# Two attention layers and 32 routed experts on one core: routing one turn earlier, and the last three sequences in an order of their own

## The chip, the cores and the metric

The kernel runs on one core of a Trainium2 chip. The metric is the time of one execution on the device in microseconds (us), lower is better. The engines of the core are named as in the profile: PE is TensorE (PEld its weight loads), DVE is VectorE, ACT is ScalarE, POOL is GpSimd and SP is SyncE, which here only issues DMAs. They run side by side, each through a list of instructions of its own, and wait for each other by semaphores that count up.

## The reference

A decoder layer on 16 sequences of 256 tokens with 256 values each, in float32:

```python
def reference(x, ctx_1024, ...):               # x, ctx: (16, 256, 256) float32
    # attention 1, one head
    q, k, v = x @ Wq.T + bq, x @ Wk.T + bk, x @ Wv.T + bv
    qk = einsum('bsd,btd->bst', q, k)
    theta = 0.5 + 0.2 * sigmoid(qk) + 0.15 * tanh(qk) + 0.1 * relu(qk)
    x1 = layernorm(x + (softmax(theta) @ v) @ Wo.T + bo)
    # attention 2 against ctx, 16 heads of 16, in chunks of 64 positions
    ...
    x2 = layernorm(x1 + out @ out_proj_w.T + out_proj_b)
    # feed-forward: 32 experts in 4 groups, 4 chosen per token, and a shared one
    scores = sigmoid(x2 @ router_weight.T)
    # best 2 groups by the sum of their top 2 scores, then the best 4 experts in them
    topk_w = scores[chosen] / sum(scores[chosen]) * 2.5
    mixed = sum_k topk_w[k] * (silu(x2 @ gate_w[k].T) * (x2 @ up_w[k].T)) @ down_w[k].T
    shared = (silu(x2 @ sg.T) * (x2 @ su.T)) @ sd.T
    return layernorm(x2 + mixed + shared)
```

## The kernel before

**Two halves.** The first half takes the 16 sequences through both attentions, the shared expert's first product and the routing; each token's row is written four times, once per chosen expert, into a list in memory (`routed`). Then tables are made that say which rows belong to which block (`vec_tables`, `pe_tables`). The second half runs 140 blocks of rows through the experts (`pe_gu`, `pe_down`), scatters the results to `y` and adds up and normalizes them (`vec_out`). The change is in the first half and in the tables; from the first expert block on the code is the same.

**Turns and lags.** The first half is a loop of turns `t` from 0 to 21. In each turn an engine does certain steps of several sequences, each with its own lag: sequence `t` gets its first attention (steps `z`, `vo`, `scores1`, `tanh`, `pr`, `prT`, `av1`, `x1`, and `k`, `v` from ctx), sequence `t-1` gets `norm1`, `x1T` and `q`, sequence `t-2` its second attention (`scores2`, `mxa`, `sha`, `mxb`, `shb`, `pTa`, `pTb`, `den`, `av2`, `rden`, `spread`, `o`, `out2`, `x2`). `x2` is DVE's sum and statistics before the second layernorm. Sequence `t-3` gets `rs2` on POOL (the inverse root) and `norm2` on ACT, late in the turn. Sequence `t-4` is routed: `x2T` (transposes on PE, L339, then a copy on ACT), `router` (L538), `sc`, `route`, `choice`, `rank` (L563), `key`, and `gate` (L547) with `hs1`; sequence `t-5` gets `up` (L556) and `hs2`, and the eight scatters of a sequence (`scattera`, `scatterb`, POOL) follow at lags of 5 and 6. A step named with a number, `key(15)`, is that step of that sequence. Turns 0 to 15 start new sequences; turns 16 to 21 only drain, here called the tail. `live(i)` leaves out what lies outside 0 to 15.

**What sets the order.** Each engine has its own list, written out by hand in the loop bodies (PE L733 to L783, ACT L956 to L996, DVE L1292 to L1337, POOL L1394 to L1406). Within an engine nothing overtakes (PE may only load weights early). So a step starts when the one ahead of it on its engine is through and its semaphores have arrived. PSUM banks are shared between steps: `vo` and `gate`, `av2` and `out2` use bank 6, `x2T`, `router` and `up` bank 7, `z`, `scores1`, `prT` and `rank` bank 5, `scores2` banks 0 to 3. For that reason there are waits such as `after(e, SEM["v_ve2"], i - 2)` in `pe_vo`: bank 6 must have been read by `x2` of sequence `t-3`.

**The end of the half.** `vec_tables` starts when `pe_tables` has counted the rows; that matmul waits for `key(15)` and `hs2(15)`. The blocks' loads on SP wait for the tables and for all scatters to have landed.

## Time and profile before

| | us |
|---|---|
| median of 3 runs | 793.93 |
| lowest, highest | 793.92, 798.06 |
| the profiled execution | 795.5 |
| its span | 793.6 |
| TensorE busy | 742.6 (94%) |
| VectorE busy | 564.5 (71%) |
| ScalarE busy | 476.0 (60%) |
| GpSimd busy | 349.8 (44%) |

Times inside the profile are counted from the start of its span; 1.9 us of the execution lie around the span. In the span the turns 0 to 15 end at 409.66 (where `scores2(14)` starts), the tail ends with `key(15)`, and the first expert block's matmuls start at 493.04.
### The profile page before, as it was taken

What the parts mean: (1) busy time and instruction counts of PE and PEld (TensorE: products, weight loads), DVE (VectorE), ACT (ScalarE), POOL (GpSimd) and SP (SyncE); (2) the same over time, 40 slices, a digit from 0 to 9 for tenths busy, and PEclk for the clock granted to TensorE, in tenths of its full rate; (3) what the DMA queues carried; (4) which work ended last, traced back from release to release, by engine and by line L of the source; (5) the groups of instructions that cost most, each with busy time, mean ns of one, the idle gap of its engine ahead of it and who ended that gap; (6) DMA issues with size and microseconds to landing.
All of it is one profiled execution on the core that took longest, in us unless ns stands there. A gap on an engine that the chain in (4) does not pass through costs nothing.

```text
span 793.6 us, 21763 instructions
## 1 busy us (share of the span) xinstructions
PE 742.6 (94%) x8276; PEld 627.1 (79%) x8276; DVE 564.5 (71%) x2038; ACT 476.0 (60%) x1110; POOL 349.8 (44%) x418
## 2 busy tenths in 40 slices
...
GB/s 257 158 100 58 65 98 88 133 122 115 136 136 120 132 117 126 123 124 133 82 51 106 141 103 120 248 273 262 280 301 277 274 271 266 246 222 102 391 402 236
DMA packets 75884, 138.84 MB, mean 175 GB/s; under 512 B 10882, under 2 KB 42114, under 8 KB 75651
## 3 DMA queue, kind: packets, MB, share of 16 engines
...
q10 hardware_dynamic: 4368, 4.20, 1.5%
...
## 4 chain that ended last, share of the span: by engine, by line
PE 82%; DVE 7%; DMA 5%; issue 2%; SPq 2%; ACT 2%; POOL 1%; ACTq 0%; DVEq 0%
PE banks L604 13%; PE banks L339 11%; PE banks L624 7%; PE banks L412 4%; PE banks L444 4%; PE banks L547 3%; PE banks L389 3%; PE banks L435 3%; PE banks L380 3%; PE banks L425 3%; PE banks L556 3%; PE banks L521 3%; PE banks L397 3%; DMA w_expert_tile<-y 2%; PE banks L513 2%; PE banks L487 2%
## 5 line engine op out<-in xcount | busy, mean ns | idle before, releaser
L1409 POOL DMA_INDIRECT y<-yb_tile,idcol_tile x140 | 134.2, 959 | 106.5 <-DVE yb_tile L1257 99.1
L604 PE MATMUL banks<-xbT_tile,wgu_tile 128*128 128x128 f32 x1024 | 136.6, 277 | 0.0
L604 PEld LDWEIGHTS banks<-xbT_tile,wgu_tile 128*128 128x128 f32 x1024 | 125.7, 193 | 0.4 <-ACT xbT_tile L809 0.3
L1257 DVE SCALAR_TENSOR_TENSOR yb_tile<-banks,rowsb_tile 128x256 f32<-128x256 f32 x140 | 67.7, 484 | 80.6 <-PE banks L624 52.7
L948 ACT ACTIVATE wgu_tile<-w_expert_tile 128x512 f32 x128 | 79.8, 623 | 24.2 <-DVE tab_i_tile L1232 17.3
L1387 POOL DMA_INDIRECT routed<-row_tile,idx_tile x64 | 62.5, 977 | 67.3 <-PE banks L457 51.8
L624 PE MATMUL banks<-w_expert_tile,hb_tile 128*128 x256 | 78.4, 388 | 0.7 <-DVE hb_tile L1244 0.6
L936 ACT ACTIVATE gb_tile<-banks 128x128 f32<-128x128 f32 x140 | 38.8, 277 | 63.5 <-PE banks L604 57.0
L1381 POOL DMA_INDIRECT routed<-row_tile,idx_tile x64 | 61.6, 963 | 33.8 <-issue 18.5
L1362 POOL TENSOR_TENSOR rs_tile<-ve_tile,half_neg_tile 128x2 f32<-128x2 f32 x16 | 11.1, 693 | 143.5 <-DVE ve_tile L1051 143.5
L809 ACT ACTIVATE xbT_tile<-banks 128x256 f32<-128x256 f32 x140 | 52.9, 378 | 9.3 <-PE banks L339 7.3
L339 PE MATMUL banks<-const_tile,rowsb_tile 128*128 128x128 f32 x280 | 55.0, 279 | 2.1 <-DMA rowsb_tile<-routed 2.1
L339 PEld LDWEIGHTS banks<-const_tile,rowsb_tile 128*128 128x128 f32 x280 | 38.3, 142 | 20.8 <-issue 6.2
L722 ACT ACTIVATE w_expert_tile<-w_expert_tile,fnmr_tile,frs_tile 128x256 f32<-128x256 f32 x32 | 17.6, 593 | 49.1 <-DVE fnmr_tile L702 49.1
L624 PEld LDWEIGHTS banks<-w_expert_tile,hb_tile 128*128 128x128 f32 x256 | 38.7, 191 | 6.8 <-issue 6.6
L1244 DVE TENSOR_TENSOR hb_tile<-hb_tile,banks 128x128 f32<-128x128 f32 x140 | 40.1, 287 | 4.8
L1241 DVE SCALAR_TENSOR_TENSOR hb_tile<-gb_tile,banks 128x128 f32<-128x128 f32 x140 | 39.3, 281 | 3.8 <-ACT gb_tile L936 3.8
L1357 POOL TENSOR_TENSOR xc_tile<-x_sb_tile,c_out_tile 128x256 f32<-128x256 f32 x32 | 22.6, 733 | 42.7 <-ACT x_tile L901 22.5
L715 POOL TENSOR_TENSOR frs_tile<-fve_tile,fhalf_tile 128x2 f32<-128x2 f32 (+1 forms) x17 | 17.9, 1055 | 43.2 <-DVE fve_tile L697 43.2
L556 PE MATMUL banks<-x2T_tile,w_early_tile 128*128 128x256 f32 x128 | 35.1, 423 | 1.3 <-ACT sc_tile L921 1.3
L679 PE MATMUL banks<-w_expert_tile,const_tile 128*128 128x512 f32 (+1 forms) x68 | 30.6, 577 | 4.2 <-DMA w_expert_tile<-y 4.1
L444 PE MATMUL banks<-w_expert_tile,w_early_tile 128*128 128x256 f32 x128 | 32.0, 391 | 0.2 <-issue 0.2
...
## 6 DMA issues: line engine op xcount, KB each, us to landing
...
rowsb_tile<-routed SPq DMA_DIRECT2D x128, 129.0 KB
...
```

Of the source, the lines that this page charges most:

```text
L339: return e.transpose(o, i, ident)
L444: m = e.matmul(bank[0][:, db * S:(db + 1) * S], w_cross[:, k, 0, db * P:(db + 1) * P], x1T[:, k, :], start=k == 0, stop=k == DK - 1)
L556: m = e.matmul(bank[7][:, b * S:(b + 1) * S], w_shared_in[:, k, 2 * P + b * P:3 * P + b * P], x2T[i % 2][:, k, :], start=k == 0, stop=k == ...
L604: m = e.matmul(o[:, h * P:(h + 1) * P], wgu[s % WG][:, k * D + h * EI:k * D + (h + 1) * EI], xbT[s % 2][:, k * P:(k + 1) * P], start=k == ...
L624: m = e.matmul(o[:, 0:D], hb[s % 4][:, :], w_flat[:, bass.ds(w.pop(g) + 2 * D, D)], start=True, stop=True)
L809: e.activation(o, i, ACT.Copy).then_inc(SEM[done], 1)
L948: e.activation(wgu[s % WG][:, :], w_flat[:, bass.ds(w.pop(n), DK * D)], ACT.Copy)
L1244: e.tensor_tensor(hb[s % 4][:, :], hb1[s % 2][:, :], bank[2 + s % 4][:, EI:2 * EI], ALU.mult)\
L1257: e.scalar_tensor_tensor(yb[s % YS][:, :], bank[6 + s % 2][:, 0:D], rowsb[s % ROWS][:, D:D + 1], rowsb[s % ROWS][:, 0:D], ALU.mult, ALU.ad ...
L1381: e.indirect_dma_start(routed, bass.IndirectOffsetOnAxis(ap=idx[i % 2][:, 0, k:k + 1], axis=0), row[i % 2][:, k, 0, :], None).then_inc(SEM ...
L1387: e.indirect_dma_start(routed, bass.IndirectOffsetOnAxis(ap=idx[i % 2][:, 1, k:k + 1], axis=0), row[i % 2][:, k, 1, :], None).then_inc(SEM ...
L1409: e.indirect_dma_start(y, bass.IndirectOffsetOnAxis(ap=idcol[n % ROWS][:, :], axis=0), yb[n % YS][:, :], None).then_inc(SEM[f"st_y{n % YS} ...
```

## The change

**Lag three.** In turns 0 to 15 all that follows the second attention moves up. `norm2(t-3)` becomes ACT's first step of the turn, `x2T`, `router`, `gate`, `up`, `rank` and the steps on DVE take sequence `t-3` instead of `t-4` (`up` and `hs2` instead of `t-5`), the scatters take `t-4` and `t-5`. POOL does `rs2(t-3)` first. On ACT `norm1(t-1)` moves from ahead of `sha` to behind `shb`. `pe_x1T` gets a wait for `a_x1`, `pe_av2` waits for the latest `hs1`, `pe_gate` and `pe_up` lose waits that their new places make needless.

**The tail written out.** The loop ends at turn 15. What is left of the last three sequences, A = 13, B = 14 and C = 15, stands behind it as a list for each engine. `x1T(15)` and `q(15)` go to banks 4 and 5. The tables' first matmul becomes `pe_counts`, which sums `macc` and `msel` itself, so it no longer waits for `key(15)` and `hs2(15)`; the tables use banks 2 and 3. `hs1(15)` and `hs2(15)` go into `vec_tables` on DVE, `up(15)` stands on PE between `pe_counts` and the tables' second matmul. The semaphore of the stores of `hs` is split in two, and SP's list is cut in the same way. The core of the diff:

```diff
         def pe_x1T(e, i):
+            e.wait_ge(SEM["a_x1"], i + 1)
+            if i == C:
+                e.wait_ge(SEM["a_v"], nseq)
+            o = bank[4 if i == C else 0]
...
         def pe_av2(e, i):
-            after(e, SEM["v_h1"], i - 1)
+            after(e, SEM["v_h1"], i)
...
         def pe_gate(e, i):
-            after(e, SEM["a_vo"], min(i + 5, nseq))
-            after(e, SEM["v_ve2"], min(i + 2, nseq))
+            after(e, SEM["a_vo"], min(i + 4, nseq))
...
         def pe_up(e, i):
-            after(e, SEM["a_sc"], min(i + 2, nseq))
-            after(e, SEM["v_hs"], i)
+            e.wait_ge(SEM["a_sc"], i + 1)
...
+        def pe_counts(e):
+            e.matmul(bank[3][0:E, 0:1], macc[:, T - 1, :], c("ones")[:, 0:1], start=True, stop=False)
+            e.matmul(bank[3][0:E, 0:1], msel[:, T - 1, :], c("ones")[:, 0:1], start=False, stop=True)\
+                .then_inc(SEM["p_tab"], 1)
+
         def pe_tables(e):
 
-            e.wait_ge(SEM["v_key"], nseq)
-            e.wait_ge(SEM["v_hs"], nseq)
-            e.matmul(bank[7][0:E, 0:1], macc[:, 0, :], c("ones")[:, 0:1], start=True, stop=True)\
-                .then_inc(SEM["p_tab"], 1)
             e.wait_ge(SEM["v_place"], 1)
...
-            for t in range(nseq + 6):
+            for t in range(nseq):
                 if live(t - 2):
                     pe_scores2(e, t - 2)
-                if live(t - 4):
-                    pe_x2T(e, t - 4)
                 if live(t):
                     pe_z(e, t)
-                if live(t - 4):
-                    pe_router(e, t - 4)
...
+            pe_scores2(e, B)
+            pe_x1T(e, C)
+            pe_x2T(e, A)
+            pe_q(e, C)
+            pe_router(e, A)
+            pe_gate(e, A)
+            pe_pTa(e, B)
+            pe_up(e, A)
...
+            pe_out2(e, B)
+            pe_scores2(e, C)
+            pe_x2T(e, B)
+            pe_router(e, B)
+            pe_gate(e, B)
+            pe_pTa(e, C)
+            pe_pTb(e, C)
+            pe_up(e, B)
+            pe_den(e, C)
...
+            pe_out2(e, C)
+            pe_rank(e, B)
+            pe_x2T(e, C)
+            pe_router(e, C)
+            pe_gate(e, C)
+            pe_rank(e, C)
+            pe_counts(e)
+            pe_up(e, C)
             pe_tables(e)
...
+            act_norm1(e, C)
+            act_norm2(e, A)
+            act_x1T(e, C)
+            act_sha(e, B)
...
+            act_norm2(e, B)
+            act_sha(e, C)
+            act_x2T(e, B)
...
+            vec_hs1(e, C, ch)
             e.wait_ge(SEM["p_tab"], 2)
...
+            vec_hs2(e, C, ch)
             e.wait_ge(SEM["p_tab"], 4)
...
+            vec_route(e, B, ch)
+            vec_rden(e, C, ch)
+            vec_hs1(e, B, ch)
+            vec_route2(e, B, ch)
+            vec_o(e, C, ch)
+            vec_choice(e, B, ch)
+            vec_hs2(e, B, ch)
+            vec_x2(e, C, ch)
+            vec_key(e, B, ch)
+            vec_route(e, C, ch)
+            vec_route2(e, C, ch)
+            vec_choice(e, C, ch)
+            vec_key(e, C, ch)
             vec_tables(e, ch)
...
+            for t in range(nseq):
                 if live(t - 3):
                     pool_rs2(e, t - 3)
+                if live(t - 5):
+                    pool_scatterb(e, t - 5)
+                if live(t - 4):
+                    pool_scattera(e, t - 4)
```

Left out are the rest of the lists, the bank numbers in the tables, and the split semaphore.

**ScalarE, from the last steps of one steady turn into the next.** L915 (after: L958) is `norm2`, L873 (L915) `q`, L832 (L874) `v`, L809 on x2T (L851) its copy, L814 (L856) `z`, L921 `sc`, L901 `norm1`, L879 (L922) `sha`. Before:

```order
L915 ACTIVATE x20_tile<-xc20_tile,nmr20_tile,rs20_tile 128x256 x2
L873 ACTIVATE qT_tile<-banks,b_cross_tile 128x256 x2
L832 ACTIVATE vM1_tile<-banks 64x8x16 x8
L809 ACTIVATE x2T0_tile<-banks 128x512
L814 ACTIVATE zT_tile<-banks,g_bias_tile 128x256 x2
L921 ACTIVATE sc_tile<-banks 128x64
L901 ACTIVATE x11_tile<-xc_tile,nmr1_tile,rs1_tile 128x256 x2
L879 ACTIVATE sha_tile<-sha_tile 128x1024
```

After:

```order
L915 ACTIVATE qT_tile<-banks,b_cross_tile 128x256 x2
L874 ACTIVATE vM1_tile<-banks 64x8x16 x8
L958 ACTIVATE x21_tile<-xc21_tile,nmr21_tile,rs21_tile 128x256 x2
L856 ACTIVATE zT_tile<-banks,g_bias_tile 128x256 x2
L922 ACTIVATE sha_tile<-sha_tile 128x1024
L851 ACTIVATE x2T1_tile<-banks 128x512
L883 ACTIVATE vo_tile<-banks 128x256 x2
```

`norm2` went from ahead of `q` and `v` of the turn before to the place between `v` and `z`, and `norm1` and `sc` left the stretch ahead of `sha`.

**TensorE, the start of turn 14.** L457 (after: L466) is `scores2`, L339 (L341) on x2 is `x2T`, L380 (L382) `z`, L538 (L547) `router`, L389 (L391) `vo`, L397 (L399) `scores1`, L556 (L563) `up`, L555 is `gate`. Before:

```order
L457 MATMUL banks<-kM0_tile,qT_tile 64x128 x32
L339 MATMUL banks<-const_tile,x20_tile 128x128 x4
L380 MATMUL banks<-xT_tile,g_qk_tile 128x256 x4
L538 MATMUL banks<-w_router_tile,x2T0_tile 128x32 x4
L389 MATMUL banks<-g_vo_tile,xT_tile 128x257 x4
L397 MATMUL banks<-xT_tile,zT_tile 128x256 x4
L556 MATMUL banks<-x2T1_tile,w_early_tile 128x256 x4
```

After:

```order
L466 MATMUL banks<-kM0_tile,qT_tile 64x128 x32
L382 MATMUL banks<-xT_tile,g_qk_tile 128x256 x4
L391 MATMUL banks<-g_vo_tile,xT_tile 128x257 x4
L341 MATMUL banks<-const_tile,x21_tile 128x128 x4
L399 MATMUL banks<-xT_tile,zT_tile 128x256 x4
L547 MATMUL banks<-w_router_tile,x2T1_tile 128x32 x4
L341 MATMUL banks<-const_tile,sha_tile 128x128 x8
L555 MATMUL banks<-x2T1_tile,w_early_tile 128x256 x4
L563 MATMUL banks<-x2T1_tile,w_early_tile 128x256 x4
```

`x2T` went behind `vo`, `router` behind `scores1`, and `up` behind `gate`, which are now of the same sequence.

**TensorE, the tail, from `scores2(15)` on.** Names as above; L339 (L341) on sha and shb are `pTa(15)` and `pTb(15)`. Before:

```order
L457 MATMUL banks<-w_expert_tile,qT_tile 64x128 x32
L339 MATMUL banks<-const_tile,x21_tile 128x128 x4
L538 MATMUL banks<-w_router_tile,x2T1_tile 128x32 x4
L556 MATMUL banks<-x2T0_tile,w_early_tile 128x256 x4
L339 MATMUL banks<-const_tile,sha_tile 128x128 x8
L547 MATMUL banks<-x2T1_tile,w_early_tile 128x256 x4
L339 MATMUL banks<-const_tile,shb_tile 128x128 x8
```

After:

```order
L466 MATMUL banks<-w_expert_tile,qT_tile 64x128 x32
L341 MATMUL banks<-const_tile,x20_tile 128x128 x4
L547 MATMUL banks<-w_router_tile,x2T0_tile 128x32 x4
L555 MATMUL banks<-x2T0_tile,w_early_tile 128x256 x4
L341 MATMUL banks<-const_tile,sha_tile 128x128 x8
L341 MATMUL banks<-const_tile,shb_tile 128x128 x8
L563 MATMUL banks<-x2T0_tile,w_early_tile 128x256 x4
```

Ahead of `pTa(15)` there now stand `x2T`, `router` and `gate` of sequence 14, where before there were `x2T` and `router` of 13 and `up` of 12, and `up(14)` stands between `pTb(15)` and the `den` that follows.

## Rows read from the trace of the kernel before

**Rows 1.** Busy time by stretch: turns 3, 4 and 15 (first: the columns).
```profile
core 0: us, PE busy (x) PEld busy (x) DVE busy (x) ACT busy (x) POOL busy (x), PEclk, DMA share, GB/s
65.04:89.72 24.68, 21.72 (x353) 18.57 (x352) 13.42 (x31) 15.89 (x38) 4.51 (x8) 1.00 0.24 82
...
89.72:117.14 27.42, 25.14 (x378) 21.85 (x377) 20.42 (x76) 19.59 (x44) 4.51 (x8) 1.00 0.23 74
...
383.28:409.66 26.38, 26.38 (x386) 23.33 (x385) 23.24 (x81) 18.52 (x40) 12.32 (x16) 1.00 0.17 59
```

**Rows 2.** Timeline, TensorE, turn 13: start, duration, engine, line, tile, count [idle before].
```profile
329.64 1.21 PE L457 MATMUL banks<-w_expert_tile,qT_tile 32*64 32x128 f32 x64
330.77 0.66 PE L339 MATMUL banks<-const_tile,x_tile 128*128 128x128 f32 x4
331.27 1.89 PE L380 MATMUL banks<-xT_tile,g_qk_tile 128*128 128x256 f32 x8
333.00 0.97 PE L538 MATMUL banks<-w_router_tile,x2T_tile 128*128 128x32 f32 x8
333.81 1.98 PE L389 MATMUL banks<-g_vo_tile,xT_tile 128*128 128x257 f32 x8
335.63 1.89 PE L397 MATMUL banks<-xT_tile,zT_tile 128*128 128x256 f32 x8
337.35 1.89 PE L556 MATMUL banks<-x2T_tile,w_early_tile 128*128 128x256 f32 x8
```

**Rows 3.** Timeline, TensorE, turn 3: the spread, with the idle time inside it.
```profile
85.73 0.42 PE L513 MATMUL banks<-rden_tile,const_tile 128*32 128x64 f32 x12 [1.65 <-issue]
```

**Rows 4.** Timeline, VectorE, start of turn 13: last step of x2's statistics.
```profile
332.29 0.17 DVE L1051 TENSOR_SCALAR ve_tile<-ag_tile 128x2 f32<-128x2 f32 x1
```

**Rows 5.** Timeline, GpSimd, turn 12: rs2 and nmr2.
```profile
316.80 0.76 POOL L1368 TENSOR_TENSOR rs_tile<-ve_tile,half_neg_tile 128x2 f32<-128x2 f32 x1
317.64 0.20 POOL L1370 TENSOR_TENSOR nmr_tile<-neg_tile,rs_tile 128x2 f32<-128x2 f32 x1
```

**Rows 6.** Timeline, ScalarE: norm2 in turn 11, z in turn 13.
```profile
299.71 1.10 ACT L915 ACTIVATE x_tile<-xc_tile,nmr_tile,rs_tile 128x256 f32<-128x256 f32 x2
...
333.20 0.84 ACT L814 ACTIVATE zT_tile<-banks,g_bias_tile 128x256 f32<-128x256 f32 x2 [1.13 <-PE banks L380]
```

**Rows 7.** Timeline, ScalarE, turn 16: copy of the first transposed shares, exp of the second.
```profile
418.49 1.02 ACT L887 ACTIVATE sha_tile<-banks 128x1024 f32<-128x1024 f32 x1 [2.55 <-PE banks L339]
419.42 1.05 ACT L883 ACTIVATE shb_tile<-shb_tile 128x1024 f32<-128x1024 f32 x1
```

**Rows 8.** Busy time by stretch: turn 16, turn 17, the drain in two pieces.
```profile
409.66:430.09 20.43, 16.27 (x326) 13.58 (x325) 16.87 (x63) 11.94 (x21) 10.03 (x12) 1.00 0.20 71
430.09:449.07 18.98, 14.46 (x314) 11.99 (x314) 16.64 (x62) 8.73 (x11) 13.95 (x16) 1.00 0.38 129
449.07:461.28 12.21, 7.99 (x34) 6.38 (x32) 9.47 (x51) 4.20 (x6) 8.68 (x10) 0.79 0.48 159
461.28:479.94 18.66, 13.56 (x42) 10.39 (x43) 11.87 (x62) 3.22 (x4) 8.96 (x11) 0.59 0.26 93
```

**Rows 9.** Timeline, TensorE: first transposes of turn 17; rank of sequence 14.
```profile
437.83 1.06 PE L339 MATMUL banks<-const_tile,sha_tile 128*128 128x128 f32 x8 [1.88 <-DVE shb_tile L1082]
...
460.37 0.69 PE L563 MATMUL banks<-msel_tile,const_tile 128*128 128x64 f32 x2 [3.22 <-DVE wraw_tile L1150]
```

**Rows 10.** Timeline, VectorE: routing of sequence 14; last instruction of key(15).
```profile
452.08 0.19 DVE L1106 TENSOR_SCALAR sc_tile<-sc_tile 128x64 f32<-128x64 f32 x1
...
456.07 0.18 DVE L1135 MATCH_REPLACE8 er_tile<-ev_tile,tmp_tile 128x36 f32<-128x36 f32 x1
...
458.42 0.33 DVE L1141 TENSOR_SCALAR msel_tile<-er_tile 128x64 f32<-128x64 f32 x1
...
477.72 0.42 DVE L1188 TENSOR_REDUCE row_tile<-mine_tile 128x8 f32<-128x256 f32 x1
```

**Rows 11.** Timeline, GpSimd: the last scatter of sequence 15.
```profile
487.25 0.96 POOL L1387 DMA_INDIRECT routed<-row_tile,idx_tile  x1 [0.30 <-issue]
```

**Rows 12.** Timeline, TensorE: the first expert block.
```profile
493.04 1.26 PE L339 MATMUL banks<-const_tile,rowsb_tile 128*128 128x128 f32 x4 [2.12 <-DMA rowsb_tile<-routed]
```

More of the change, by code:

```diff
@@ L863, in act_x1T @@
             e.wait_ge(SEM["p_x1T"], i + 1)
-            copy(e, x1T[:, :, :].rearrange("p a b -> p (a b)"), bank[0][:, :], "a_x1T")
+            copy(e, x1T[:, :, :].rearrange("p a b -> p (a b)"), bank[4 if i == C else 0][:, :], "a_x1T")
         def act_x2T(e, i):
@@ L996, in _ @@
                     act_v(e, t)
+            act_norm1(e, C)
+            act_norm2(e, A)
+            act_x1T(e, C)
+            act_sha(e, B)
+            act_x2T(e, A)
+            act_q(e, C)
+            act_sc(e, A)
+            act_pTa(e, B)
+            act_shb(e, B)
+            act_gates(e, A)
+            act_pTb(e, B)
+            act_row(e, A)
+            act_num(e, B)
+            act_norm2(e, B)
+            act_sha(e, C)
+            act_x2T(e, B)
+            act_sc(e, B)
+            act_pTa(e, C)
+            act_shb(e, C)
+            act_gates(e, B)
+            act_pTb(e, C)
+            act_num(e, C)
+            act_row(e, B)
+            act_norm2(e, C)
+            act_x2T(e, C)
+            act_sc(e, C)
+            act_gates(e, C)
+            act_row(e, C)
             e.wait_ge(SEM["v_tab"], 1)
@@ L1204, in vec_tables @@
             e.tensor_scalar(rows_full[:, :], place[:, E:E + 1], float(P), None, ALU.mult)
+            vec_hs1(e, C, ch)
             e.wait_ge(SEM["p_tab"], 2)
-            ch(e.tensor_scalar(above[:, :], bank[7][0:E, 8:8 + E], order[:, 0:1], None, ALU.is_gt))
+            ch(e.tensor_scalar(above[:, :], bank[3][0:E, 8:8 + E], order[:, 0:1], None, ALU.is_gt))
             ch(e.tensor_reduce(rank[:, :], above[:, :], AX.X, ALU.add))
-            ch(e.tensor_tensor(rank[:, :], bank[7][0:E, 8 + E:9 + E], rank[:, :], ALU.add))
+            ch(e.tensor_tensor(rank[:, :], bank[3][0:E, 8 + E:9 + E], rank[:, :], ALU.add))
             ch(e.scalar_tensor_tensor(nblk[:, 1:2], rank[:, :], float(FULL), over[:, :], ALU.is_ge, ALU.mult))
@@ L1290, in _ @@
             e.tensor_copy(c_bqbk[:, :], bank[2][:, 0:1]).then_inc(SEM["v_setup"], 1)
-            for t in range(nseq + 6):
+            for t in range(nseq):
                 if live(t - 2):
@@ L1465, in _ @@
             e.dma_start(w_shared_out[:, :, :], d["w_shared_out"]).then_inc(SEM["ld_w"], 16)
-            for t in range(nseq + 6):
+            for t in range(nseq):
                 if live(t) and t > 0:
@@ L1474, in _ @@
                     load_c(e, t)
-                if live(t - 6):
-                    store_hs(e, t - 6)
+                if live(t - 4):
+                    store_hs(e, t - 4)
                 if 0 < t <= nseq - LATE:
                     load_rest(e, t - 1)
-                if nseq < t <= nseq + LATE:
-                    load_rest(e, t - 1 - LATE)
+            store_zero(e, B)
+            store_zero(e, C)
+            store_hs(e, A - 1)
+            store_hs(e, A)
+            for i in range(nseq - LATE, nseq):
+                load_rest(e, i)
+            store_hs(e, B)
+            store_hs(e, C)
             e.wait_ge(SEM["v_adr"], 1)
```

165 lines of the change are left out of this document (109 added, 56 removed).

## The prediction

> **What bounds the kernel now.** I read the busy times by stretch first. In a steady turn TensorE has no idle time at all: turn 15 is 26.38 us long and 26.38 us busy, at the full clock, while VectorE has 3.1 us to spare, ScalarE 7.9 and GpSimd 14.1 [rows 1]. Two kinds of stretch are different. Turns 3 and 4 have 2.96 and 2.28 us of TensorE idle time, because routing has not begun or `up` is missing [rows 1]. And the tail, from 409.66 to the end of `key(15)` at 477.72 + 0.42 = 478.14 [rows 8, 10], takes 68.5 us for some 50 us of TensorE time, part of it at the half clock: PEclk is 0.79 and 0.59 in the drain [rows 8]. Behind `key(15)` come its eight scatters, the last issued at 487.25 [rows 11], then the first block's matmuls at 493.04 [rows 12], 14.9 us after `key(15)`. From there on nothing changes. So the change is worth what it does to two lengths: turns 2 to 15, and the tail up to `key(15)`.
>
> **Part 1: work goes from the tail into the turns.** Turn 3 gets a whole routing: `x2T` 0.50, `router` 0.81, `gate` and `up` 1.73 each (the starts of the rows that follow each other [rows 2]), `rank` about 0.4, so 5.2 us; turn 4 gets one `up`, 1.7. Turn 3 will be as long as a full turn, 26.4, plus what idle time stays. Of its 2.96 us, 1.65 is a pause inside the spread that has no releaser [rows 3]; I keep it. The other 1.3 is filled. That makes 28.0 for 24.68, **+3.3**. Turn 4: 26.4 plus a like pause of 1.65 makes 28.0 for 27.42, **+0.6**. A turn that is bound by TensorE hides nothing of this. It would be free only if the tail gets shorter by as much.
>
> **Part 2: the chain at the start of each turn.** This is the term I weigh most. At lag four `norm2` had most of a turn of slack. At lag three it must run at once. Counted from the start of `scores2`, 329.64 [rows 2]: the statistics of x2 end at 332.29 + 0.17 = 332.46, so +2.8 [rows 4]. That does not move, as it hangs on `rank` and `key` at the end of the turn before. Then GpSimd's two steps, 316.80 to 317.84, 1.04 [rows 5]: +3.9. ScalarE stands in front of `norm2` from then on, 1.10 [rows 6]: +5.0. Behind `norm2` in its queue is `z`, 0.84 [rows 6], which before began at 333.20 = +3.6 and now begins at about +4.9, as adjacent ScalarE instructions overlap by 0.1: done at +5.7. TensorE meanwhile has `scores2` 1.13, `z` 1.73, `vo` 1.82, through at +4.7 [rows 2]. It waits for `norm2` until +5.0 (0.3), does `x2T` until +5.5, and waits for `z` until +5.8 (0.25) before `scores1`. So about 0.6 us of TensorE idle time in each of turns 3 to 15: 13 x 0.6 = **+7.8**. Behind `scores1` I find no further wait: `router` has its copy of x2T at about +7.2 and starts at +7.5; `norm1` is done by about +12.5 and `x1T` starts at +14.4. The bounds: 0 if GpSimd and ScalarE come 0.6 us earlier than these rows say; 1.2 a turn (+15.6) if `vo`, whose wait for the same statistics at +2.8 falls within 0.1 us of its turn at +2.9, is late as well and each hand-over costs 0.1 more.
>
> In turn 2 nothing is routed and TensorE is early, so that `norm1` behind the copy and the exp of the shares, 1.02 and 1.05 [rows 7], makes `x1T` late: between 0 and 2.1, I take **+1.0**. The sum of the turns: 3.3 + 0.6 + 7.8 + 1.0 = **+12.7**.
>
> **Part 3: the tail.** I lay it out in three legs against before [rows 8].
>
> Leg 1, `scores2(14)` to `scores2(15)`: 20.43 before. Now `x1T(15)` goes early but its copy stands behind `norm2(13)` on ScalarE (+5.0, then 0.6), and from +5.0 the engines alternate: 5.7 us of TensorE work (`x2T`, `q`, `router`, `gate`, `pTa`), copy and exp of the shares (2.1, [rows 7]), transposes, copy, `den`, `rden`, `choice`, `o`, `out2` end at about +21.1. **+0.7**.
>
> Leg 2, `scores2(15)` to the end of `x2(15)`: before 430.09 to 452.1, 22.0 [rows 8, 10]. Then `pTa(15)` started 7.7 after `scores2(15)`, when VectorE's shares were there [rows 9]. Now ahead of it stand `x2T(14)`, which must wait for statistics, GpSimd and `norm2(14)` (+6.4 in the leg), the copy behind `sha(15)` (+8.2), `router` and `gate`, so `pTa(15)` starts at about +10.7; and `up(14)`, 1.73, stands between `pTb(15)` and `den`, where ScalarE's copy (1.0) would hide but part. The leg takes about 25.8: **+3.8**.
>
> Leg 3, end of `x2(15)` to the end of `key(15)`: 452.1 to 478.14, 26.0. In it sequence 14 is routed first and 15 after. Now 15 goes directly: GpSimd 1.04 and `norm2` 1.10 [rows 5, 6]; `x2T` to the start of routing as 449.07 to 452.08, 3.0; routing 452.08 to 456.25, 4.2; `choice` to `rank` 458.42 to 460.37, 1.95 [rows 8 to 10]; `rank` and `key` to the end about 3.7 by the same steps before, at the half clock. Sum 15.0, and 0.9 for a `router` at the half clock: 15.9. **-10.1**.
>
> So the legs give 0.7 + 3.8 - 10.1 = -5.6, with legs 1 and 2 at the full clock. I do not believe in that clock. Before, the clock went down in the drain and the engine met a 3.22 us gap that ended at half speed [rows 8, 9]. By my layout the new tail has gaps of about 3 us behind `x1T(15)`, 5.3 behind `scores2(15)`, 3.3 ahead of `x2T(15)`. Each of the first two should cost some 2 us (about 4 us of work at half speed until the clock is back), and the work between `pTb(15)` and `out2(15)`, 6.6 us, may fall low as well: between 0 and 6.6, I take 1.5. **+5.5**, bounds 0 and 10.6. The tail is then -0.1, about as long as before. The Trainium skill's page "TensorE: Matmul & The Clock Gate", Part 1, says that the throttled state is the default and that activity releases it; the trace agrees so far that PEclk is 1.00 only where the engine is kept busy. By that rule the gaps cost what I add here; if it did not hold the tail would be the 5.6 us shorter.
>
> **Part 4: the tables.** `counts` no longer waits for `hs2(15)`, and `hs1(15)`, `hs2(15)` fill waits. That would bring the tables some 1.9 us forward from `key(15)`. I cost it at nothing, because the eight scatters of sequence 15 cannot start before `key(15)`: the last is issued 9.1 us after it [rows 10, 11] and must land before SP loads. The 14.9 us stay. If the tables were the later of the two, up to 1.9 would be won.
>
> **The sum.** 12.7 in the turns and -0.1 in the tail, +12.6. The profiled execution's 795.5 becomes 808.1. It lay 1.6 above the median of 793.93, so the median should come to **806.5**.
>
> **The rivals.**
> *A, no stall at the turn's start* (0.10): the chain of part 2 fits into its slack. For it: 0.6 us is a small difference of rows that are each 0.1 wide. Against: three engines in series without any reserve. 806.5 - 7.8 = 798.7.
> *B, the clock stays up in the tail* (0.08): legs 1 and 2 lose nothing, leg 3 some 2 less. 806.5 - 7.5 = 799.0. For it: in turn 17, with 14.46 of 18.98 us busy, PEclk was 1.00 [rows 8]. Against: gaps of 5 us were not in that turn.
> *C, faster: the written-out tail is bound by TensorE's work and not by hand-overs* (0.08). Its place is legs 1 and 2: if the new order covers every hand-over, they take no more than TensorE was busy in turns 16 and 17, 16.27 and 14.46 us [rows 8], in place of 46.9, and the clock stays up. The tail is 30.7 + 15.9 = 46.6, which is 21.9 shorter: 793.9 + 12.7 - 21.9 = 784.7. It decides from a tail under 55.8 us, where it outweighs the turns. For it: 18 us of the old tail were idle on TensorE. Against: each sequence's second attention goes through seven hand-overs, and only two sequences are left to alternate.
> *D, a worse stall*, 1.2 us a turn (0.08): 814.3.
> *E, the shift does nothing*: turns stay at 26.4 and the tail gains what turns 3 and 4 lose. It lands within 4 us of 793.93 (0.06).
>
> **How the numbers follow.** The forecast, 806.5, with its own bounds of 801 to 813, has 0.60. 0.5% is 4 us, about what a measurement of this kernel can tell from no change. Faster than 790: C and a little from E and the unseen, 0.10. Within: E, parts of A and B, 0.12. Slower than 798: the forecast, D and the larger part of A and B, 0.78. A range from 796 to 815 leaves out C, E and the far ends.
>
> **What would show it.** In the profile after: the start of `scores2(14)` at about 422 instead of 409.66; turns of 27.0; on TensorE a wait of 0.2 to 0.4 for `z` ahead of `scores1` and another for `norm2` in each turn; from there to the end of `key(15)` about 68 us, with PEclk below 1 already in the first half of it; 14.9 us from `key(15)` to the first block. Turns of 26.4 would make part 2 wrong; a tail of under 60 us would make part 3 wrong; a first block nearer than 13.5 us to `key(15)`, part 4.

## The result and the profile after

| | before | after |
|---|---|---|
| median | 795.22 us (4 runs beside after, 793.92 to 798.06) | 809.44 us (4 runs, 805.82 to 811.79) |
| ratio | | 1.0166, 95% interval 1.0139 to 1.0192 |
| span of the profiled execution | 793.6 us | 807.9 us |
| start of `scores2(14)`, end of the turns | 409.66 | 422.34 |
| from there to the end of `key(15)`, the tail | 68.48 us | 70.47 us |
| end of `key(15)` to the first expert block | 14.90 us | 14.88 us |

The change makes the kernel slower by 1.7%. In the two profiled executions 12.7 us of it lie in the turns, 2.0 in the tail, and nothing behind it. First the turns. Busy time by stretch, kernel after, turns 2, 3, 4 and 15 (columns as in [rows 1]); turns 3, 4 and 15 answer to the rows of before there:

```profile
43.34:66.90 23.56, 21.89 (x352) 18.63 (x353) 11.14 (x24) 15.62 (x39) 4.46 (x8) 1.00 0.28 86
66.90:93.96 27.06, 26.63 (x385) 23.40 (x385) 21.56 (x77) 19.22 (x44) 4.56 (x8) 1.00 0.23 64
93.96:121.85 27.89, 27.23 (x385) 23.32 (x385) 22.31 (x81) 18.84 (x42) 8.65 (x12) 1.00 0.31 101
...
395.24:422.34 27.10, 26.93 (x386) 23.19 (x385) 23.08 (x81) 18.79 (x42) 12.80 (x16) 1.00 0.17 61
```

Turn 15 is 27.10 us long instead of 26.38, with the same 385 or 386 matmuls. Its 0.17 us of idle time does not show this; the starts do. Timeline of TensorE, start of turn 15 (columns as in [rows 2]), and of ScalarE:

```profile
395.24 1.21 PE L466 MATMUL banks<-w_expert_tile,qT_tile 32*64 32x128 f32 x64
396.38 1.99 PE L382 MATMUL banks<-xT_tile,g_qk_tile 128*128 128x256 f32 x8
398.21 1.98 PE L391 MATMUL banks<-g_vo_tile,xT_tile 128*128 128x257 f32 x8
400.28 0.66 PE L341 MATMUL banks<-const_tile,x_tile 128*128 128x128 f32 x4
401.00 1.99 PE L399 MATMUL banks<-xT_tile,zT_tile 128*128 128x256 f32 x8
```
```profile
399.14 1.09 ACT L958 ACTIVATE x_tile<-xc_tile,nmr_tile,rs_tile 128x256 f32<-128x256 f32 x2 [3.35 <-POOL nmr_tile L1476]
400.14 0.82 ACT L856 ACTIVATE zT_tile<-banks,g_bias_tile 128x256 f32<-128x256 f32 x2
```

`vo` holds TensorE for 1.82 us [rows 2], so it is free at 400.03; `x2T` starts at 400.28, 5.04 into the turn, when `norm2` is done. `x2T` holds it for 0.50, until 400.78; `scores1` starts at 401.00, when `z` is done. Of the two waits, 0.25 and 0.22 us, the profile's idle column shows only 0.17, because the ends of matmuls are modelled. One has to subtract starts. Done for every step of turn 15 in both kernels, this gives the whole difference: `vo` and `x2T` with the waits behind them 0.25 and 0.23, `z` 0.10 (1.83 where it follows `scores2`, 1.73 where it followed `x2T`), `scores1` 0.11, `pTa` 0.03, together 0.72.

The tail, busy time by stretch: leg 1 (turn 16's place), leg 2 with the wait for `x2T(15)`, leg 3:

```profile
422.34:447.30 24.96, 19.09 (x325) 15.86 (x324) 17.04 (x62) 11.47 (x19) 15.29 (x18) 0.86 0.21 74
447.30:479.18 31.88, 18.38 (x313) 15.27 (x312) 18.75 (x74) 9.83 (x13) 9.57 (x12) 0.81 0.26 94
479.18:492.81 13.63, 10.31 (x34) 8.07 (x35) 7.75 (x49) 3.22 (x4) 7.80 (x8) 0.50 0.23 80
```

Against [rows 8]: PEclk was 1.00 in both stretches before, and is 0.86 and 0.81 now. TensorE's rows that set the legs:

```profile
427.38 1.11 PE L341 MATMUL banks<-const_tile,x_tile 128*128 128x128 f32 x4 [2.80 <-ACT x_tile L958]
428.29 3.62 PE L453 MATMUL banks<-w_expert_tile,w_early_tile 128*128 128x256 f32 x8
...
443.88 0.72 PE L522 MATMUL banks<-rden_tile,const_tile 128*32 128x64 f32 x34 [1.05 <-issue]
...
452.57 0.66 PE L341 MATMUL banks<-const_tile,x_tile 128*128 128x128 f32 x4 [4.06 <-ACT x_tile L958]
454.33 1.91 PE L547 MATMUL banks<-w_router_tile,x2T_tile 128*128 128x32 f32 x8 [1.11 <-ACT x2T_tile L851]
456.06 3.76 PE L555 MATMUL banks<-x2T_tile,w_early_tile 128*128 128x256 f32 x8
459.61 1.32 PE L341 MATMUL banks<-const_tile,sha_tile 128*128 128x128 f32 x8
462.99 1.44 PE L341 MATMUL banks<-const_tile,shb_tile 128*128 128x128 f32 x8 [2.06 <-ACT shb_tile L926]
464.22 3.27 PE L563 MATMUL banks<-x2T_tile,w_early_tile 128*128 128x256 f32 x8
...
479.18 1.12 PE L341 MATMUL banks<-const_tile,x_tile 128*128 128x128 f32 x4 [4.02 <-ACT x_tile L958]
```

There are three waits for `norm2` (L958), of 2.80, 4.06 and 4.02 us, and behind each the engine runs at its lower level: `q(15)` (L453) takes 3.4 us and `gate(14)` (L555) 3.55, where at the full clock they take 1.83 and 1.73. `pTa(15)` starts 12.3 us into leg 2 (before: 7.7, [rows 9]).

The end: last step of `key(15)`, last scatter, first block, against [rows 10 to 12].

```profile
492.39 0.42 DVE L1261 TENSOR_REDUCE row_tile<-mine_tile 128x8 f32<-128x256 f32 x1
```
```profile
501.94 0.96 POOL L1498 DMA_INDIRECT routed<-row_tile,idx_tile  x1 [0.30 <-issue]
```
```profile
507.69 1.12 PE L341 MATMUL banks<-const_tile,rowsb_tile 128*128 128x128 f32 x4 [4.04 <-DMA rowsb_tile<-routed]
```

### The profile page after: what moved, and what is told of

Same layout as the page of the kernel before. It is cut to its first block, busy times and chain, and to the rows that moved or that the text cites. A ratio compares the mean times of both kernels' runs of the same rounds, so it can differ in the third digit from the quotient of the medians.

```text
span 807.9 us, 21741 instructions
## 1 busy us (share of the span) xinstructions
PE 752.2 (93%) x8278; PEld 629.0 (78%) x8278; DVE 563.8 (70%) x2038; ACT 473.4 (59%) x1110; POOL 355.4 (44%) x418
## 3 DMA queue, kind: packets, MB, share of 16 engines
q0 software_dynamic: 12864, 35.28, 11.7%
## 4 chain that ended last, share of the span: by engine, by line
PE 71%; DVE 12%; ACT 5%; DMA 5%; POOL 3%; issue 3%; SPq 1%; ACTq 0%; POOLq 0%; DVEq 0%
PE banks L614 12%; PE banks L341 10%; PE banks L634 7%; PE banks L453 4%; PE banks L399 4%; PE banks L414 4%; PE banks L555 3%; PE banks L431 3%; PE banks L563 3%; PE banks L441 3%; DMA w_expert_tile<-y 2%; PE banks L522 2%; PE banks L496 2%; PE banks L510 2%; PE banks L547 2%
## 5 line engine op out<-in xcount | busy, mean ns | idle before, releaser
L991 ACT ACTIVATE wgu_tile<-w_expert_tile 128x512 f32 x128 | 79.8, 623 | 22.6 <-issue 22.6
L1491 POOL DMA_INDIRECT routed<-row_tile,idx_tile x64 | 66.9, 1045 | 24.3 <-issue 19.3
L1498 POOL DMA_INDIRECT routed<-row_tile,idx_tile x64 | 62.4, 975 | 17.8 <-issue 17.8
L851 ACT ACTIVATE xbT_tile<-banks 128x256 f32<-128x256 f32 x140 | 52.9, 378 | 10.7 <-PE banks L341 8.7
L1468 POOL TENSOR_TENSOR rs_tile<-ve_tile,half_neg_tile 128x2 f32<-128x2 f32 x16 | 11.4, 716 | 107.9 <-DVE ve_tile L1122 107.9
L341 PE MATMUL banks<-const_tile,rowsb_tile 128*128 128x128 f32 x280 | 54.8, 279 | 4.3 <-DMA rowsb_tile<-routed 4.0
L341 PEld LDWEIGHTS banks<-const_tile,rowsb_tile 128*128 128x128 f32 x280 | 38.3, 142 | 22.8 <-issue 6.5
L1474 POOL TENSOR_TENSOR rs_tile<-ve_tile,half_neg_tile 128x2 f32<-128x2 f32 x16 | 11.1, 692 | 99.4 <-DVE ve_tile L1122 99.4
L958 ACT ACTIVATE x_tile<-xc_tile,nmr_tile,rs_tile 128x256 f32<-128x256 f32 x32 | 17.5, 593 | 57.4 <-POOL nmr_tile L1476 57.4
L341 PE MATMUL banks<-const_tile,x_tile 128*128 128x128 f32 x128 | 21.1, 290 | 14.7 <-ACT x_tile L958 10.9
```

Of the source, the lines that this page charges most:

```text
L341: return e.transpose(o, i, ident)
L851: e.activation(o, i, ACT.Copy).then_inc(SEM[done], 1)
L991: e.activation(wgu[s % WG][:, :], w_flat[:, bass.ds(w.pop(n), DK * D)], ACT.Copy)
L1491: e.indirect_dma_start(routed, bass.IndirectOffsetOnAxis(ap=idx[i % 2][:, 0, k:k + 1], axis=0), row[i % 2][:, k, 0, :], None).then_inc(SEM ...
L1498: e.indirect_dma_start(routed, bass.IndirectOffsetOnAxis(ap=idx[i % 2][:, 1, k:k + 1], axis=0), row[i % 2][:, k, 1, :], None).then_inc(SEM ...
```

## The experiments

The experiments ran in three groups; the runs of a group share one chip. Group 1 has no run of the kernel after. The kernel before was slower there than in the comparison: its median in the groups was 822.24, 827.39 and 826.77 us. Ratios are against the kernel before in the same group; legs are compared inside a group where that is possible. Leg 1 goes from `scores2(14)` to `scores2(15)`, leg 2 to the end of the statistics of `x2(15)`, leg 3 to the end of `key(15)`.

| run | ratio, interval | steady turn | leg 1 | leg 2 | leg 3 |
|---|---|---|---|---|---|
| before, compared | 1 | 26.4 to 27.0 | 20.43 | 22.1 | 26.0 |
| after, compared | 1.0166 | 27.10 | 24.96 | 29.6 | 15.9 |
| group 1: e1 | 1.0098 (1.0059 to 1.0137) | 27.2 to 27.3 | 30.8 | 30.1 | 15.9 |
| e2 | 1.0522 (1.0459 to 1.0585) | 28.8 to 32.6 | | | |
| e3 | 1.0106 (1.0067 to 1.0145) | 27.10 | 31.4 | 31.2 | 18.5 |
| e4 | 1.0002 (0.9980 to 1.0025) | 27.10 | 25.6 | 26.5 | 19.6 |
| group 2: after | 1.0097 (1.0064 to 1.0131) | 27.6 | 31.1 | 32.8 | 15.9 |
| e5 | 1.0027 (1.0006 to 1.0049) | 27.6 | 26.4 | 25.4 | 20.1 |
| e6 | 1.0135 (1.0095 to 1.0174) | 27.7 | 31.8 | 30.6 | 18.6 |
| e7 | 1.0041 (1.0023 to 1.0059) | 27.3 to 28.0 | 22.9 | 29.1 | 24.6 |
| group 3: before | one run, 823.83 | 27.3 to 27.9 | 21.6 | 28.7 | 25.5 |
| after | 1.0092 (1.0055 to 1.0129) | 27.5 to 27.6 | 32.1 | 30.2 | 15.9 |
| e8 | 1.0129 (1.0102 to 1.0155) | 27.75 | 27.5 | 27.1 | 20.9 |
| e9 | 1.0095 (1.0061 to 1.0129) | 27.5 to 27.6 | 31.4 | 30.2 | 15.4 |

**e2: is `norm2` on the path of every turn?** Each `norm2` is written in pieces:

```diff
-                m = e.activation(x2[i % 2][:, t, :], xc2[i % 2][:, t, :], ...)
+                n = D // 4 if i < A else D
+                for a in range(0, D, n):
+                    m = e.activation(x2[i % 2][:, t, a:a + n], xc2[i % 2][:, t, a:a + n], ...)
```

> The kernel after, with norm2 of sequences 0 to 12 written as eight instructions of 64 columns in place of two of 256. The result is the same; ScalarE takes some 1 us more for it, if one small instruction costs about 0.27 us (an estimate from the 1.10 us of the two and the 0.2 us that the smallest instructions on that engine take in the traces). Chain theory: norm2 is on the path in each of the 13 turns, so each steady turn grows by the whole added time, about 1 us, from 27.1 to 28.1, +13 us in all, and the wait that the profile names is x2T's for norm2. Order theory: there is slack at that place, and the turns grow by less than half of what is added.

Turn 13 of e2, ScalarE's `norm2` and TensorE's `x2T`:

```profile
376.14 2.76 ACT L960 ACTIVATE x_tile<-xc_tile,nmr_tile,rs_tile 128x64 f32<-128x64 f32 x8 [3.35 <-POOL nmr_tile L1478]
```
```profile
378.95 0.66 PE L341 MATMUL banks<-const_tile,x_tile 128*128 128x128 f32 x4 [1.77 <-ACT x_tile L960]
```

`norm2` takes 2.76 instead of 1.09 us, 1.67 more (I had guessed 1), and the turn is 28.77 instead of the 27.10 of e3 and e4 on that chip: 1.67 more. That is one to one, without slack, so the chain theory holds. Turn 15 is as long (28.79). The other turns from 5 on are 0.7 to 3.8 us longer still; in most of them ScalarE pauses up to 4.1 us with no releaser, so the run's 5% is not a measure of the step alone.

**e1: `z` ahead of `norm2`.**

```diff
+                if live(t):
+                    act_z(e, t)
                 if live(t - 3):
                     act_norm2(e, t - 3)
-                if live(t):
-                    act_z(e, t)
```

> The kernel after, with one change: on ScalarE, in the loop, the step z stands ahead of norm2 and no longer behind it. Chain theory (in a steady turn TensorE waits twice at the turn's start, for norm2 ahead of x2T and for z ahead of scores1, because GpSimd, norm2 and z run in series): z is done a microsecond earlier and the wait ahead of scores1 goes, 0.22 to 0.25 us a turn; norm2 comes no earlier, so x2T still waits. A steady turn goes from 27.10 to about 26.9 us, and the run is 2 to 4 us shorter than the kernel after, ratio to the kernel before about 1.013. Order theory (the 0.5 us that a steady turn has grown comes from the matmuls' new order or from VectorE's added steps, not from these two waits): turns stay at 27.10, 0 us. If norm2 is late instead of z, x2T waits longer and the turn grows.

ScalarE and TensorE, turn 12 of e1, which begins at 314.61:

```profile
317.78 0.84 ACT L856 ACTIVATE zT_tile<-banks,g_bias_tile 128x256 f32<-128x256 f32 x2 [2.62 <-PE banks L382]
318.51 1.09 ACT L958 ACTIVATE x_tile<-xc_tile,nmr_tile,rs_tile 128x256 f32<-128x256 f32 x2
```
```profile
319.65 0.66 PE L341 MATMUL banks<-const_tile,x_tile 128*128 128x128 f32 x4
320.15 1.89 PE L399 MATMUL banks<-xT_tile,zT_tile 128*128 128x256 f32 x8
321.88 0.97 PE L547 MATMUL banks<-w_router_tile,x2T_tile 128*128 128x32 f32 x8
322.78 1.06 PE L341 MATMUL banks<-const_tile,sha_tile 128*128 128x128 f32 x8
```

`x2T` starts 5.04 into the turn, as before this edit, and `scores1` right behind it at 5.54 instead of 5.76: the wait for `z` is gone, the one for `norm2` stays, as the theory said. `pTa` starts at 8.17 instead of 8.41. But the turn is no shorter: 27.2 to 27.3 against 27.10 in e3 and e4. The gain is lost in `pTb`, which starts at 14.75 instead of 14.99 and then stops behind its first transpose, with no releaser:

```profile
329.36 0.27 PE L341 MATMUL banks<-const_tile,shb_tile 128*128 128x128 f32 x1
329.93 0.92 PE L341 MATMUL banks<-const_tile,shb_tile 128*128 128x128 f32 x7 [0.30 <-issue]
```

By the starts, each of the turns 5 to 15 of e1 loses 0.3 to 0.5 us here, and none of e3 and e4 on the same chip does. Less this pause and the one in the spread, the turns of e1 are 26.8 to 26.9 us, the expected 26.9. So the edit is worth what the theory says, 0.24 a turn, and a pause takes it back; whether the edit or the chip brings the pause is not shown. In microseconds of the run the expectation missed, as far as it can be told without the kernel after on that chip.

**e8: no wait for the chain at all, and the loop running on.** It has e4's loop (below), and in it:

```diff
-scores2, z, vo, x2T, scores1, router, pTa, gate ...     (TensorE)
+scores2, z, vo, scores1, x2T, pTa, router, gate ...
-norm2, z, sha, x2T, vo, tanh ...                        (ScalarE)
+z, norm2, sha, vo, x2T, tanh ...
```

> Lag three with the loop running on (the kernel of e4), and the start of the turn re-ordered: TensorE scores2, z, vo, scores1, x2T, pTa, router in place of scores2, z, vo, x2T, scores1, router, pTa; ScalarE z, norm2, sha, vo, x2T, tanh in place of norm2, z, sha, x2T, vo, tanh. In the last three turns zero matmuls fill the waits ahead of x2T(13), x2T(14), x2T(15) and rank(15) (7, 7, 9 and 5 of them). Chain theory: nothing on TensorE waits for the chain rs2, norm2 any more, so a steady turn is 0.4 to 0.6 us shorter than the kernel after's on the same chip, 6 to 8 us over the turns; with pTa ahead of router and the clock kept up, legs 1 and 2 take 22 to 24 us each; the run is 0.5 to 1% shorter than the kernel before, ratio 0.990 to 0.995. Order theory (the half microsecond has another cause, such as tanh and sc a little later in the turn): turns as long as in the kernel after, ratio 0.999 to 1.004.

TensorE at the start of turn 13 of e8, and VectorE's last step of the shares:

```profile
352.94 0.60 PE L341 MATMUL banks<-const_tile,x_tile 128*128 128x128 f32 x4
354.61 1.06 PE L341 MATMUL banks<-const_tile,sha_tile 128*128 128x128 f32 x8 [1.07 <-issue]
```
```profile
353.25 1.21 DVE L1096 TENSOR_TENSOR shb_tile<-banks,mxb_tile 128x1024 f32<-128x1024 f32 x1
```

The turn begins at 346.44. `scores1` and `x2T` run without a wait, `x2T` is through 0.5 us after 352.94, and then `pTa` must wait for the shares, which VectorE has ready at 354.46, 8.0 us into the turn, as in both kernels. Two waits of 0.47 us together have become one of 1.17, counted by the starts in both cases. `pTa` starts at 8.17, no earlier than in e1. The turn is 27.75 us, longer than the 27.5 to 27.6 of the kernel after beside it, and the run is 1.29% slower than before: a miss. Between the end of `vo` at 4.77 and the start of `pTa` at 8.17 TensorE needs 3.4 us of work whose inputs are there; `scores1` and `x2T` are 2.2. `v` would be such work and was not tried there.

**e4 and e5: the shift without the written-out tail.** The lists behind the loops are taken out, the loops run to `nseq + 5`, and `hs1(15)`, `hs2(15)` go from the tables back into the loop.

> The shift alone: lag three as in the kernel after, but the loop runs on for the last sequences in its own order, as in the kernel before, and nothing is written out. Turns 0 to 15 should be those of the kernel after: scores2(14) at 422. Theory that the written-out order costs (gate(14) and up(14) ahead of pTa(15) and den(15), copies behind norm2): here pTa comes ahead of gate, so leg 1 is about 21.3 us (after: 24.96), leg 2 about 24 (29.6) and leg 3 about 16 (15.9), a tail of 61 where after has 70.5 and before 68.5; the run is about +5 us against before, ratio 1.006, and some 9 us shorter than after. Theory that the written-out order is what shortens the tail: leg 3 stays near before's 26 us and the run is about +13 to +20, ratio 1.017 to 1.025.

> The kernel of e4 again (lag three, the loop runs on, nothing written out), beside the kernel after. Theory that the written-out order costs: ratio to before 0.998 to 1.006, ratio to after 0.985 to 0.990, with leg 1 at 21 to 22 us where after has 25.0, leg 2 at 24 to 26.5 where after has 29.6, leg 3 at 16 to 19. Theory that e4's 1.0002 was a matter of its chip: the same ratio to before as the kernel after, 1.017.

Tail of e5, and of the kernel after beside it:

```profile
427.25:453.61 26.36, 19.43 (x326) 16.69 (x325) 16.55 (x63) 11.58 (x19) 10.05 (x12) 0.81 0.15 53
453.61:478.96 25.35, 16.09 (x313) 13.90 (x312) 19.55 (x73) 8.89 (x11) 10.08 (x12) 0.85 0.35 115
478.96:499.01 20.05, 9.29 (x36) 7.46 (x36) 8.82 (x51) 4.31 (x6) 12.51 (x14) 0.67 0.26 94
```
```profile
426.71:457.83 31.12, 17.82 (x325) 15.31 (x324) 16.27 (x62) 11.42 (x19) 15.24 (x18) 0.84 0.17 59
457.83:490.65 32.82, 20.28 (x313) 16.68 (x312) 16.71 (x65) 8.77 (x11) 8.66 (x10) 0.74 0.25 91
490.65:506.53 15.88, 10.30 (x34) 8.05 (x35) 9.79 (x58) 4.31 (x6) 8.71 (x10) 0.53 0.19 69
```

The loop's own order takes 71.8 us where the written-out one takes 79.8; the run is 830.22 us against 835.76. Legs 1 and 2 are 12.2 us shorter, leg 3 is 4.2 longer. There `hs1(15)` and `hs2(15)` stand ahead of `choice` and `key` again, 0.9 and 1.1 us, the second beside a wait for `rank`. That is the smaller part: from `choice(15)` on VectorE also stands still eight times between steps of its own, 0.2 to 0.9 us each and 3.9 in all, for instance

```profile
490.82 0.19 DVE L1151 TENSOR_TENSOR macc_tile<-macc_tile,msel_tile 128x32 f32<-128x32 f32 x1 [0.53 <-DVE msel_tile L1149]
497.20 0.29 DVE L1181 MAX8 slot_tile<-key_tile 128x8 f32<-128x32 f32 x2 [0.94 <-DVE key_tile L1179]
```

In the kernel after such steps follow each other in 0.03 us. What makes these gaps is open, so that the loop's order must lose its third leg is not shown. Not all of the 12.2 belongs to the order: ScalarE pauses in legs 1 and 2 of the kernel after, and on the chip of the comparison these legs are 9.4 us shorter. Against that trace e5's legs 1 and 2 are 2.9 us shorter and its third 4 us longer; what the loop's order would give on that chip was not run. The lag alone costs no measurable time in e4 (1.0002) and 0.3% in e5, on chips where the turns of the kernel before are longer too (below).

**e3, e6 and e9: the clock.** Matmuls of a zero tile fill TensorE's gaps in the written-out tail:

```diff
+            if i >= A:
+                fill(e, bank[7], (10, 15, 15)[i - A])     # e9: 5, 8, 8
             e.wait_ge(SEM["a_x2"], i + 1)
```

> The kernel after, with matmuls of a zero tile put into TensorE's gaps of the tail: 10, 15 and 15 of them ahead of x2T of sequences 13, 14 and 15, 8 ahead of pTb(15) and 8 ahead of rank(15), each into a bank that the next step overwrites. Clock theory: the gaps brought the clock down (q(15) took 3.4 us, gate(14) 3.55, up(14) 3.27, router(14) 1.7 and router(15) 1.7, each about half of that at the full clock). With the gaps filled these steps take their full-clock times: leg 1 is 1.5 to 2 us shorter than 24.96, leg 2 4 to 5 us shorter than 29.6, leg 3 1 to 2 us shorter than 15.88; the run is 6 to 9 us shorter than the kernel after, ratio to before about 1.007. Hand-over theory (the tail is bound by the hand-overs between engines, and the slow matmuls lie beside them): under 2 us. Fillers that outlast a gap would add up to 0.5 us each.

> The kernel of e3 again (zero matmuls in TensorE's gaps of the written-out tail), beside the kernel after. Clock theory: gate(14), up(14), router(14) and q(15) at their full-clock times; legs 1 and 2 together 4 to 6 us shorter than in the kernel after, the run 5 to 8 us shorter. Hand-over theory, to which e3 leaned (all matmuls at the full clock, and still a leg 2 of 31.2 us to the end of x2(15)): the tail is no more than 2 us shorter, or longer by what the fillers outlast their gaps.

> The kernel after with fillers of the right size: in e3 and e6 15 of them took 6.7 us at the full clock (0.45 us each), 2 to 3 us more than the waits they stood in. Now 5, 8 and 8 ahead of x2T(13), (14), (15), 3 ahead of pTb(15) and 8 ahead of rank(15), none longer than its wait. Clock theory: leg 2 is 4 to 5 us shorter than in the kernel after on the same chip, leg 3 about 1 us shorter, leg 1 up to 1.5 us, the run 5 to 7 us. Hand-over theory: under 2 us.

In e3 and e6 15 fillers took 6.7 us and outlasted their gaps by 2 to 3, so leg 3 grew to 18.5 us, and the run was no faster. Only e9 can be read. Its legs by stretch, and three rows of its leg 2, which begins at 457.95:

```profile
426.56:457.95 31.39, 20.39 (x335) 17.42 (x334) 16.26 (x62) 11.43 (x19) 15.28 (x18) 0.84 0.17 59
457.95:488.16 30.21, 22.24 (x344) 18.54 (x344) 16.80 (x65) 8.74 (x11) 8.69 (x10) 0.94 0.29 99
488.16:503.53 15.37, 11.62 (x61) 9.22 (x59) 9.82 (x59) 4.31 (x6) 8.72 (x10) 1.00 0.19 70
```
```profile
467.70 1.04 PE L341 MATMUL banks<-const_tile,sha_tile 128*128 128x128 f32 x8
```
```profile
472.20 1.02 ACT L940 ACTIVATE sha_tile<-banks 128x1024 f32<-128x1024 f32 x1 [5.89 <-remote]
```

PEclk is 0.94 and 1.00 in legs 2 and 3, where the kernel after beside it has 0.77 and 0.54. The Trainium skill ("TensorE: Matmul & The Clock Gate", Part 1) has it that activity releases the throttle; zero matmuls did, the trace agrees. `pTa(15)` starts 9.75 us into leg 2; in the kernel after beside it 12.35, in the compared one 12.3. So the half clock costs 2.6 us up to there on this chip. But the copy that follows on ScalarE starts at 14.25 in e9 and at 14.3 in the kernel after beside it. There it starts as the transposes end; in e9 they end 3.5 us earlier, and ScalarE has a pause with no releaser just there. Leg 2 is 30.2 us in both. Leg 3 gains 0.5. The clock's price is seen in TensorE's rows; that removing it saves time was not shown on these chips. In the kernel after of the comparison the same copy starts at 13.67, as its transposes end, without such a pause; there the fillers were not run.

**e7: the kernel before with only its drain written out.** Lag four stays; behind turn 17:

```diff
+x2T(14) router(14) up(13) gate(14) x2T(15) router(15) rank(14) up(14) gate(15) rank(15) up(15)   (TensorE)
+scatterb(12) rs2(15) scattera(13) scatterb(13) scattera(14) ...                                 (GpSimd)
```

> The kernel BEFORE, lag four, with its drain alone written out: turns 0 to 17 as they are; then norm2 and x2T of sequence 15 go ahead of rank(14) (in another bank, the scores in another buffer), rs2(15) goes ahead of eight scatters on GpSimd, and up(15) ahead of the tables. Leg theory (of the change only leg 3 is worth having, and it can be had without lag three): the end of key(15) comes from x2's statistics at +21 us instead of +26.0, the last scatter is then bound by GpSimd at about 483.5 us of the span instead of 487.25; the run is 3 to 5 us shorter than before, ratio 0.994 to 0.996. Rival: GpSimd's 20 scatters in a row from x2(15) on are the bound already, and the run gains under 1.5 us, ratio 0.998 or more.

Two rows of its tail, TensorE's `x2T(15)` and VectorE in the tables:

```profile
479.80 1.09 PE L343 MATMUL banks<-const_tile,x_tile 128*128 128x128 f32 x4 [3.81 <-issue]
```
```profile
510.17 0.33 DVE L1251 TENSOR_SCALAR tab_tile<-banks 1x176 f32<-1x176 f32 x1 [6.61 <-remote]
```

Leg 3 is 24.6 us, where 21 was expected and the kernel before took 25.5 in group 3; the run is 0.4% slower than before, a miss. A pause of 3.81 us stands ahead of `x2T(15)`, and one of 6.61 in the tables puts the first block 19.2 us behind `key(15)`. From `key(14)` on, GpSimd issues its 16 scatters without a gap, and the last comes 9.9 us behind `key(15)` (9.1 in both kernels), so the rival is right in part: from here on GpSimd's queue binds. The experiment tells nothing on what the order would be worth without the pauses.

**The two kernels as they are.**

> The kernel after, unchanged, as the measure for the kernels beside it on this chip. The first four experiments ran on a chip on which the kernel before took 822 us, 27 more than where the two kernels were compared. If the change costs the same everywhere, the ratio to before is 1.0166 (1.0139 to 1.0192) here too, leg 1 is 25.0 us, leg 2 29.6 and leg 3 15.9. If the written-out tail meets something that depends on the chip (ScalarE's and TensorE's pauses of 1.5 to 5.5 us with no releaser, seen in the experiments' legs 1 and 2), the ratio differs and the difference stands in leg 1 or 2.

> The kernel before, unchanged, for its trace on the chip on which the kernels beside it run: ratio 1. If the pauses without a releaser that the experiments show on their chips (0.5 to 1 us in every turn, single ones of 4 to 7 us in the tail) belong to the chip and not to the change, they stand here too: turns of 27.3 to 28.0 us instead of 26.4 to 27.0, scores2(14) near 420 instead of 409.66, and one or two pauses of 4 to 7 us between 420 and 520.

> The kernel after, unchanged, beside the kernel before on one chip, so that the turns and the legs of both can be compared there. By the comparison of the two traces on the first chip: turns 2 to 15 12.7 us longer, leg 1 +4.5, leg 2 (to the end of x2's statistics) +7.6, leg 3 -10.1. By the ratio 1.0097 of the kernel after on the third chip: less than that in the turns, +6 to +8, because there the kernel before loses time to pauses that the kernel after loses anyway.

Longest waits of ScalarE's copy of the shares (us in total, times, longest), kernel before and kernel after of group 3:

```profile
ACT sha_tile L887 <- remote: 35.2, 10, 3.6
```
```profile
ACT sha_tile L930 <- remote: 33.8, 12, 8.7
```

The trace of before on the first chip has no such row. So the change does not bring the pauses: the kernel before has them too, once a turn from turn 6 on. Because of them its turns 5 to 15 average 27.41 us instead of 26.59, and TensorE waits some 0.7 for ScalarE ahead of `pTb`. The kernel after loses less by them (27.67 instead of 27.32 over the same turns). So the turns cost 8.5 us there (418.42 against 426.92) instead of 12.7. The tail costs 2.4 (75.8 against 78.2) instead of 2.0.

## Why the prediction was right

**Parts 1 and 2 together.** The sum of the turns, 12.7, is what was measured, 12.68; its terms are not, and that they cancel is luck. The 0.6 of part 2 was also counted for turns 3 and 4, so these two were to cost 3.3 + 0.6 + 1.2 = 5.1; they cost 2.38 + 0.47 = 2.85. I kept a pause of 1.65 us in the spread of each, and it shrank: the spread holds TensorE for 1.65 and 1.79 us there instead of 2.95 and 2.97 (1.01 without a pause). In turn 3 `x2T` does not wait at all. Turn 2, forecast at 1.0, costs 1.29, and 0.57 lie ahead of it. In turn 2 `x1T` waits 1.44 us for `norm1`, as laid out. Turns 5 to 15 were to cost 11 x 0.6 = 6.6 and cost 7.97.

**Part 2, the mechanism.** `x2T` was to start at 5.0 and `scores1` at 5.8 into the turn; measured 5.04 and 5.76. e2 shows that the chain has no slack. The waits of 0.25 and 0.22, and the 0.11 by which `scores1` holds TensorE longer behind its wait (in e1, without the wait, it takes 1.73 again), make 0.58, the 0.6 that was priced. The rest of the 0.72 a turn, 0.10 for `z` and 0.03 for `pTa`, comes with the new order and was at nothing in the prediction. Every turn from 5 on is 26.38 us before and 27.10 after, plus a pause in the spread with no releaser: before it is up to 0.6 us, the longest in turns 11 to 14, and 2.3 in all; after it stands in turns 5 to 7 (27.6, 27.8, 28.1) and 9, and is 2.4 in all. So 11 x 0.72 = 7.9 is the change, and the pauses are the same on either side. What makes them is open.

**Part 3.** Leg 1: forecast 21.1 and some 2 for the clock; measured 24.96. In e9 `pTa(14)` starts 9.97 into the leg at the full clock, as laid out (5.0 and 4.9 of work), in the kernel after 12.55: the clock costs 2.6 there (1.7 in the kernel after beside e9, which is at 11.62), and the spread has a 1.05 pause. Leg 2: forecast 25.8 and some 3.5 for the clock, 29.3; measured 29.6. In it `x2T(14)` starts at 5.3 instead of behind a `norm2(14)` laid out at 6.4, and the clock takes 2.6 instead of some 2 up to `pTa(15)`, so two smaller errors partly cancel. The 4 us of work at half speed that the prediction puts behind each gap come from none of the rows it names; what the runs showed is the 1.7 to 2.6 us that a leg loses by it. Leg 3: forecast 15.9, measured 15.88. The tail came out at 70.47 where 68.4 follows from the forecast: the term that was mis-sized is leg 1, by 1.9.

**Part 4.** The tables are done 9.8 us behind `key(15)` instead of 11.7, and the first block starts 14.88 instead of 14.90 behind it. The scatters bind: the last is issued 9.1 us behind `key(15)` in both kernels, and in the kernel after SyncE's waits right ahead of the blocks' loads are for them to land, the longest 4.9 us. The gain is worth nothing, as costed.

**The rivals.** A (no stall) falls by e2 and the starts. B (the clock stays up) falls by PEclk 0.86, 0.81 and 0.50. C (the tail bound by TensorE's work, under 55.8 us) falls: its tail has TensorE busy for 47.8 of 70.5 us, and hand-overs to `norm2` alone keep it idle for 10.9. D (1.2 us a turn) falls by turns of 27.10, 0.72 longer than before. E falls by the same turns. The forecast of 806.5 was 2.9 us short of 809.44. Of this 1.3 is the median of before, which came out at 795.22 beside the kernel after instead of 793.93. The other 1.6 is the tail, 2.1, less half a microsecond, 0.35 of which lies behind the start of the first block.
